# Graph layers on one Trainium2 core: the picked scores and the edge_attr vector are read from PSUM

## The reference

```python
# stage 0: two GCN convolutions with self loops, relu between, sigmoid behind
deg  = segment_sum(ew, dst);  dinv = where(deg > 0, rsqrt(deg), 0)
out  = segment_sum((x @ W)[src] * (dinv[src] * ew * dinv[dst])[:, None], dst) + b
x    = layernorm(x + gcn2(relu(gcn1(x))).sigmoid())
# stage 1: attention over the edges of a destination
z  = h @ fc_w.T;  rh = edge_attr @ fc_r_w.T
e  = z[src] @ aw[0] + z[dst] @ aw[1] + rh @ aw[2];  e = leaky_relu(e, 0.01)
alpha = softmax of e within one dst
out = relu(segment_sum(alpha[:, None] * (z[src] + rh), dst) + z @ loop_w)
x   = layernorm(x + out)
```

## Time and profile before

| what | value |
|---|---|
| median of 3 runs | 4149.51 us (4148.2 to 4155.21) |
| span of the profiled execution | 4158.1 us |
| PE / DVE / ACT / POOL busy | 44% / 38% / 4% / 54% of the span |
| picks, line 1001 | 782 pairs of instructions, 235.0 + 62.4 us busy |
| edge_attr products, line 924 | 782 pairs, 183.7 + 61.6 us busy |
| ScalarE's copies of the scores, lines 706 and 707 | 12 and 13 |

### The profile page before, as it was taken

One profiled execution on the slowest core, in us unless ns is written; L12 is line 12 of the kernel. 1 busy time (PEld: TensorE's weight loads), 2 busy tenths in 40 slices (PEclk: granted clock), 3 DMA queues, 4 the chain that ended last, 5 costly groups with the idle time before them and its releaser, 6 DMA issues. The chain is left out here.

```text
span 4158.1 us, 32695 instructions
## 1 busy us (share of the span) xinstructions
PE 1810.8 (44%) x10379; PEld 1679.2 (40%) x10379; DVE 1599.5 (38%) x7455; ACT 169.0 (4%) x291; POOL 2254.0 (54%) x2357
## 2 busy tenths in 40 slices
PE   1344544333347211443443446003555655555576
PEld 1234444323337111443333446002555555555576
DVE  3555323345447100244444458314222333233343
ACT  0000000000000000000000001000000000000000
POOL 7434666666660776666666650773555555555500
PEclk9756565655557555555555657555666666666677
DMA  3103323334344121112121110222323323332311
GB/s 105 30 24 85 79 61 93 105 111 119 106 119 122 52 53 40 49 53 52 51 53 50 52 42 12 52 55 67 81 72 81 83 75 80 76 84 75 79 57 36
DMA packets 325061, 287.99 MB, mean 69 GB/s; under 512 B 43178, under 2 KB 284769, under 8 KB 324866
## 3 DMA queue, kind: packets, MB, share of 16 engines
q0 software_dynamic: 75072, 155.50, 15.1%
q1 hardware_dynamic: 236886, 123.92, 10.4%
q10 hardware_dynamic: 12924, 6.41, 0.5%
HBM read 272.66 MB, written 13.40 MB: 69 GB/s over the span
## 5 line engine op out<-in xcount | busy, mean ns | idle before, releaser
L499 PE MATMUL ps<-SR,ring 128*128 128x128 f32 (+16 forms) x5844 | 1319.5, 367 | 1582.7 <-DVE SR L900 707.1
L372 POOL DMA_INDIRECT ring<-x_d,srcC x1404 | 1347.3, 960 | 1114.9 <-issue 402.4
L499 PEld LDWEIGHTS ps<-SR,ring 128*128 128x128 f32 x5844 | 1184.4, 283 | 1634.6 <-issue 1615.1
L372 POOL DMA_INDIRECT ring<-h_d,srcC x782 | 751.6, 961 | 484.3 <-issue 230.4
L900 DVE TENSOR_SCALAR SR<-iota,rankC,ewC 128x128 f32<-128x128 f32 x1404 | 395.4, 354 | 413.0 <-issue 247.3
L502 PE MATMUL ps<-SR 128*128 128x128 f32 (+12 forms) x1948 | 508.5, 348 | 80.2 <-issue 79.6
L502 PEld LDWEIGHTS ps<-SR 128*128 128x128 f32 x1948 | 428.1, 268 | 96.2 <-issue 96.0
L1001 DVE SCALAR_TENSOR_TENSOR U<-iota,rankC,U 128x128 f32<-128x128 f32 x782 | 235.0, 346 | 183.0 <-issue 182.5
L924 DVE SCALAR_TENSOR_TENSOR SR<-SR,v2B 128x128 f32<-128x128 f32 x782 | 183.7, 285 | 90.9 <-issue 90.8
L900 DVE TENSOR_SCALAR SR<-iota,rankC,cols 128x128 f32<-128x128 f32 x782 | 211.1, 346 | 2.0 <-issue 0.2
L372 POOL DMA_INDIRECT ring<-in_x_dram,srcC x160 | 153.2, 958 | 97.0 <-issue 48.2
(11 more groups left out here) (166 smaller groups left out, 1039.3 us busy)
## 6 DMA issues: line engine op xcount, KB each, us to landing
SR<-in_edge_attr_dram SPq DMA_DIRECT2D x194, 512.0 KB
ring<-x_d,srcC POOLq DMA_INDIRECT x1404
ring<-h_d,srcC POOLq DMA_INDIRECT x782
U<-lo_d SPq DMA_DIRECT2D x20, 256.0 KB
x_d<-rows SPq DMA_DIRECT2D x12, 264.0 KB
x_d<-rows SPq DMA_DIRECT2D x7, 448.0 KB, 5.2
rows<-in_x_dram SPq DMA_DIRECT2D x6, 512.0 KB
h_d<-rows ACTq DMA_DIRECT2D x12, 256.0 KB
```

The lines of the kernel that those rows point to most:

```text
L372: pool.indirect_dma_start(ring[:, gg % R, k, 0:width], None, (x if p == 0 and q < R0 else table)[:, :], bass.IndirectOffsetOnAxis(ap=srcC[ ...
L499: last = nc.tensor.matmul(ps[(p * NK + k) % 2][:, lo:hi], ring[:, gg % R, j, 0:D], S[:, gg % NS, j, w0:w0 + hi - lo], start=False, stop=t ...
```

## The change

The eight PSUM tensors become one, of which `ps[k]` are the banks. `s1_rows(k)` writes bank 3 + k % 4 instead of bank 3 always; for k = 4, 8 and 12 it also writes the first 128 scores of the chunk to bank 7, so that a window that begins in bank 6 can run on. ScalarE's copies and `s1B` are gone. `pick` takes its window from the banks and waits for `s1_spread` instead of `s1B_made`; TensorE waits before it writes a bank again until the picks of four chunks ago are done. `rh_dot` takes v2 from bank 7, columns 128 to 255, where DVE copies it once at the start of pass 0. The count and order of picks and products is the same.

```diff
-        s1B = U[:, 1024:1024 + 2 * (P + BW)].rearrange("p (a n) -> p a n", a=2)
-        ps = [ctx.enter_context(nc.psum_tensor(f"ps{k}", [P, BW], FP32)) for k in range(8)]
+        psum = ctx.enter_context(nc.psum_tensor("psum", [P, 8, BW], FP32))
+        ps = [psum[:, k, :] for k in range(8)]
+        banks = psum[:, :, :].rearrange("p k n -> p (k n)")
+        v2P = ps[7][:, P:2 * P]
 ...
             def s1_rows(k):
                 pe.wait_ge(s("diag_made"), k + 1)
-                if k:
-                    pe.wait_ge(s("s1B_made"), k)
+                if k >= 4:
+                    pe.wait_ge(s("picked"), sum(1 for t in range(T) if base(t) // BW <= k - 4))
                 for j, b in enumerate(blocks(k)):
-                    last = nc.tensor.matmul(ps[3][:, j * P:(j + 1) * P], ones[:, :], diag[:, j, :], start=True, stop=True)
+                    last = nc.tensor.matmul(ps[3 + k % 4][:, j * P:(j + 1) * P], ones[:, :], diag[:, j, :], start=True, stop=True)
+                if k and k % 4 == 0:
+                    last = nc.tensor.matmul(ps[7][:, 0:P], ones[:, :], diag[:, 0, :], start=True, stop=True)
                 last.then_inc(s("s1_spread"), 1)
 ...
-            pe.wait_ge(s("s1B_made"), NK)
+            pe.wait_ge(s("picked"), T)
 ...
-            def spread_s1(k):
-                n = len(blocks(k))
-                act.wait_ge(s("s1_spread"), k + 1)
-                if k >= 2:
-                    act.wait_ge(s("picked"), sum(1 for t in range(T) if (base(t) + W - 1) // BW < k - 1))
-                if k:
-                    act.wait_ge(s("s1B_made"), k)
-                    nc.scalar.copy(s1B[:, k % 2, 0:P], s1B[:, 1 - k % 2, BW:BW + P])
-                nc.scalar.copy(s1B[:, k % 2, P:P + n * P], ps[3][:, 0:n * P]).then_inc(s("s1B_made"), 1)
 ...
-                if k:
-                    spread_s1(k - 1)
-            spread_s1(NK - 1)
 ...
-                    last = v.scalar_tensor_tensor(rh[:, d % NR, j, :], rh[:, d % NR, j, :], 1.0, v2B[:, :], ALU.mult, ALU.mult,
+                    last = v.scalar_tensor_tensor(rh[:, d % NR, j, :], rh[:, d % NR, j, :], 1.0, v2P, ALU.mult, ALU.mult,
                                                   accum_out=s2C[:, t:t + 1])
 ...
+            link(v.tensor_copy(v2P, v2B[:, :]))
             lo_onehot(0)
 ...
             def pick(t):
-                k = (base(t) + W - 1) // BW
-                at = P + base(t) - k * BW
-                dve.wait_ge(s("s1B_made"), k + 1)
+                k0, k1 = base(t) // BW, (base(t) + W - 1) // BW
+                at = (3 + k0 % 4) * BW + base(t) - k0 * BW
+                dve.wait_ge(s("s1_spread"), k1 + 1)
                 if t >= NJ:
                     dve.wait_ge(s("picked"), t - NJ + 1)
-                v.scalar_tensor_tensor(junk[:, t % NJ, :], iota[:, :], rankC[:, t:t + 1], s1B[:, k % 2, at:at + W], ALU.is_equal, ALU.mult,
+                v.scalar_tensor_tensor(junk[:, t % NJ, :], iota[:, :], rankC[:, t:t + 1], banks[:, at:at + W], ALU.is_equal, ALU.mult,
                                        accum_out=s1C[:, t:t + 1]).then_inc(s("picked"), 1)
```

## The result

| kernel | median (lowest to highest) | runs |
|---|---|---|
| before | 4144.55 us (4134.57 to 4165.22) | 12 |
| after | 4166.24 us (4149.22 to 4177.95) | 12 |

The ratio of after to before is 1.0046, with a 95% interval of 1.0028 to 1.0065: the change makes the kernel 0.46% slower, some 19 us. That lies inside the predicted range (4130 to 4178) but above its bound for "no change" of 0.2%, and on the side that had a chance of 0.13.

What follows compares the result with a forecast made beforehand. It took 241 us of the critical path to be picks beside pass 2's gathers, 184 us of it an unexplained stall that stays. Terms 0 + 0 + 2 - 3 + 0 + 0.4 gave about 0: 4150 us, range 4130 to 4178.

Steps and rivals of the forecast that it cites:

- no change: Whole kernel: time within 0.2% (8 us) of before, chance 0.65.
- The stall stays: DVE picks beside pass 2's gathers: the stall remains, 0 us; bound 188 us less if all the tail's goes.
- the three points it rested on: DVE stall: follows instruction count, not kind; begins and ends later than the gathers; without gathers the same instructions run dense.
- conflict over SBUF reads: Rival for DVE beside gathers: two SBUF inputs cause the stall, so it goes; 3962 us, at most about 3780; chance 0.14.
- a buffer that fills and is drained: DVE stall beside gathers: its late beginning and late end look like this, not a port conflict; no size given.
- The operands' price: PSUM inputs of picks and products on DVE: 0 us for picks; 0, perhaps +2 us, for products.
- The bound of +59 ns a pick: Dense picks on the path: at most 59 ns dearer from PSUM, 258 picks, +15 us.
- the rival that used it: Products and picks on DVE: PSUM inputs dearer than the profile says, up to +28 us, 4178 us; chance 0.13.
- TensorE's new wait: TensorE before s1_rows(k): picks of chunk k-4 are out 15 groups before the wait, so 0 us.
- ScalarE's copies: 25 copies removed: 0 us, hidden by ScalarE idle time; at most 12 us in all if that cover were gone.
- The gathers, -3 us: GpSimd gathers in passes 0 and 1: shortened by PSUM operands, -3 us taken of a possible -28 us.
- slower by over 0.2%: Whole kernel: the slower outcome, chance 0.13, from dearer PSUM inputs, with TensorE's wait on picks below 0.01.

Runs made afterwards that it cites:

- e4: Kernel before with GpSimd's gathers of pass 2 waiting until all picks are done, on the chip with the stall: 4161.11 us, ratio 1.0042.
- e11: Kernel before with the index rows of picks and build_S (passes 0, 1) and the products' vector in PSUM, on a chip without the stall: 3115.27 us, 0.99.
- e1: The changed kernel with the products reading v2 from SBUF as before (picks' half alone), on the chip with the stall: 4164.27 us, 1.0048 against before.
- e10: Kernel before with only the picks' index row read from PSUM, repeated on a chip without the stall: 3127.2 us, ratio 0.9956.
- e9: The whole change against the kernel before, on a chip without the stall: 3122.28 us, ratio 0.9938.
- e8: Kernel before with only the picks' index row read from PSUM, scores, waits and copies kept, on a chip without the stall: 3127.16 us, ratio 0.9954.
- e5: Kernel before with one GpSimd memset of 128 columns behind every gather, on a chip without the stall: 3357.52 us, ratio 1.0689.
- e2: Kernel before with only v2 copied to PSUM and read there by the products, on the chip with the stall: 4141.97 us, ratio 0.9998.
- e3: Kernel before with picks lacking accum_out, so no accumulator reads, s1C set to 0 once, on the chip with the stall: 4186.83 us, ratio 1.0105.

## Why the prediction was right and wrong

**The stall stays: right.** This was the main term (0 of a possible -188 us), and the three points it rested on hold: after shows 14 instructions in 20 us, a first gap 9.8 us late, a stalled accumulator read. The rival "conflict over SBUF reads" (3962 us, 0.14) falls with the row of line 993: one SBUF input, the same 180 us of "issue". The reading "a buffer that fills and is drained" is borne out beyond what the prediction had: e4 moves the same stall to TensorE, and the gathers' own 1.40 us behind the 181st are what a full buffer would give.

**The operands' price, 0: right.** 343 and 283 ns against 346 and 285. The Trainium skill's "VectorE: DVE Perf Modes", section on the TRN2 errata, with its 62 cycles more for a PSUM source, is not borne out for this form; for `build_S`'s form e11 shows 39 ns. The bound of +59 ns a pick, and the rival that used it (4178 us), fall: the time came out on that rival's side, but by another way. That 4166.24 us lies inside the range is therefore luck in part: the 28 us that the range had above 4150 stood for dearer inputs alone, which did not come. The bound also counted some 50 picks of the tail behind and around the stall; 37 instructions, 18 picks, stand behind it.

**TensorE's new wait, 0: right.** In the waits of after the line of `s1_rows` has these:

```profile
PE psum L522 <- remote: 33.5, 3, 12.0
PE psum L522 <- DVE U L984: 24.5, 5, 13.2
```

Line 984 writes `diag`. "remote" means that the profile names no instruction that released the wait, so by this view alone it could be the picks. Their count excludes it: where `s1_rows(k)` starts for k = 4 to 8, the last pick that it needs was done 164 to 173 us before, and for k = 12, the closest, 32 us before. In e1 it is the same, 32 us at the closest.

**ScalarE's copies, 0: not shown apart.** On B the 5 us between e10 and e9 hold the copies, the ring and the products' operand together. They lie within the 12 us allowed, but since e11 gains 17 us by the operands of products and `build_S`, the 5 us may be the products' alone.

**The gathers, -3 us: the step that failed, in its sign.** The prediction took it that a gather shortened from 1.06 to 0.94 us can only help, a little. The shortening came as read: in pass 1 the 782 gathers are busy for 745.9 us against 751.6. On B, where gathers bound passes 0 and 1, e8 and e10 gain 0.44 to 0.46% with it; there the gathers of pass 1 take 743.0 us in e8 and 752.3 in e5, whose picks read SBUF alone (e5 has its memsets as well, and before has no trace on B). On chip A the tail's gathers take 1.40 us each from first to last, in after as in before (235.3 and 235.8 us for 168). With a start every 1.25 us instead of 1.36 beside dense picks the store would grow sooner, and DVE loses free time: 71 instructions in the 10 us before its first gap, against 93 in the 13 us before. The end of the stall stays, so more is left for afterwards: 34 instructions, 34 x 0.14 = 5 us, less 0.5 us by which the last idle piece is earlier; the tail shows 4. Of the 34, the free time accounts for 22; the others fell inside the stall.

**What is not settled.** That the loss belongs to the picks' half is shown (1.0048 against 0.9998). That the tail is 4 to 6 us longer with it is seen in two executions with picks from PSUM and two without. That the sooner handed-in gathers are the reason is argued from the order of events, not tested. The other 15 us are not placed for certain. The executions on A point to pass 1, where picks meet gathers too, and where TensorE also stands idle before `s1_rows`:

| execution | first to last gather of pass 1, us | TensorE idle before `s1_rows`, us |
|---|---|---|
| before | 1119.6 | 53.4 |
| e2, picks as before | 1109.1 | 17.8 |
| e4, picks as before | 1109.3 | 21.0 |
| after | 1120.9 | 59.0 |
| e1, picks from PSUM | 1129.7 | 79.4 |

The two with picks from PSUM are 12.6 us longer on average. But before and after differ by 1.3 us only, and executions of one kind by 9 to 10 us, so this is a direction and no proof.

The kernel that would separate the operand from the ring of banks (e8) met only chips B. There ring, missing copies and the products' operand together gain 5 us; what the ring alone costs is open on both. What serves a gather in 1.40 us on one chip and not on the others is open too.

The chances were wrong in this: "slower by over 0.2%" was filled with dearer inputs alone. A server that is already behind, which the prediction itself had read off the trace, is a reason for which a faster supplier can cost time, and it had no case.

## What to carry to other kernels

When a stall depends on the count of instructions and outlasts its cause, look for a store that fills: how long it takes to fill, how long it drains, and whether the supplier is ever held. With such a store a faster supplier gained nothing here, and moving the work beside it only handed the stall to another engine, in e3 and e4. Where a kernel is tuned for a stall, look whether other chips have it: here the same edit changes the time by +0.46% where there is a stall and by -0.62% where there is none.

## What the runs showed of the hardware

- Beside a long run of gathers, and for some 25 us behind it, chip A lets DVE and TensorE alike through one instruction per 1.40 us (matmul and weight load 2.80 us together). The chips B, with the same instructions, 17 gathers in 20 us and nearly the same DMA share, have nothing of it: 3142 against 4143 us.
- By the estimate above GpSimd gets about 19 gathers ahead of that service on chip A; from then on each of its gathers takes 1.09 us and starts 1.40 behind the last.
- A DVE instruction with two SBUF inputs lengthens a gather from 0.94 to 1.06 us and is not itself delayed: the picks had one every 0.27 us in both kernels.
- Without the accumulator reads (e3) DVE's picks ran through and held GpSimd inside a gather for the length of the tail, 39.58 of 40 us; with them a gather took 0.12 us longer. That was not expected, and no run here explains it.
